# A softmax loop with VectorE's one-operand passes gathered in one block per step, GpSimd's two passes behind it, and stages one step later

## What is computed

```python
x_int = x / scale
x_int = x_int - x_int.max(axis=-1, keepdims=True)
x_int = jnp.maximum(x_int, n * x0_int)
q = jnp.floor(x_int / x0_int)
r = x_int - x0_int * q
z = r * (r + b_int) + c_int
exp_int = jnp.clip(jnp.floor(z * jnp.exp2(n - q)), 0.0, None)
exp_sum = exp_int.sum(axis=-1, keepdims=True)
sm = jnp.round(exp_sum / exp_int)
big = jnp.floor(jnp.log2(sm))
big = jnp.where(sm - jnp.exp2(big) >= jnp.exp2(big - 1.0), big + 1.0, big)
qlog = jnp.clip(big, 0.0, float(2 ** BITS_S - 1))
return jnp.where(big >= 16, 0.0, jnp.exp2(-qlog))
...
o = jnp.einsum('bhnm,bhmd->bhnd', attn, v)
```

## Time and profile before

| | |
|---|---|
| median of three runs | 1189.9 us |
| the profiled execution | 1189.11 us, its span 1187.3 us |
| busy: TensorE / VectorE / ScalarE / GpSimd | 803.7 / 883.3 / 499.1 / 515.9 us |
| softmax loop, roughly | 434 to 695 us of the span |
| granted TensorE clock, mean of the span | 0.718 |

### The profile page before, as it was taken

The page is one execution under the profiler, slowest core; times in us unless marked ns, Lnnn a source line. Parts: engine busy times, 40 slices in busy tenths (PEclk is TensorE's granted clock), DMA queues, the critical chain, the costliest instruction groups (busy, mean ns, idle before and its releaser), DMA issues.

```text
span 1187.3 us, 25829 instructions
## 1 busy us (share of the span) xinstructions
PE 803.7 (68%) x8714; PEld 613.7 (52%) x8714; DVE 883.3 (74%) x1781; ACT 499.1 (42%) x980; POOL 515.9 (43%) x413
## 2 busy tenths in 40 slices
PE   3898961576077625777778730600739999999998
PEld 2897961455044412444445430200627777777777
DVE  4324424899689969999999976699557777777776
ACT  2222201344454314666666632120415555555554
POOL 1120002587122006666666630633007666666665
PEclk9998995778555555555555555555559999999999
DMA  7544212000022111122112134000000000000000
GB/s 201 154 119 102 63 40 82 22 1 0 12 83 69 54 28 31 28 34 33 28 33 33 21 86 140 0 0 0 10 15 16 23 22 28 28 21 20 28 21 20
DMA packets 112975, 51.84 MB, mean 44 GB/s; under 512 B 75896, under 2 KB 107808, under 8 KB 112928
## 3 DMA queue, kind: packets, MB, share of 16 engines
q1 hardware_dynamic: 111600, 44.94, 15.6%
q0 software_dynamic: 1328, 6.30, 1.9%
HBM read 26.47 MB, written 6.68 MB: 28 GB/s over the span
## 4 chain that ended last, share of the span: by engine, by line
PE 50%; DVE 24%; issue 11%; SPq 5%; DMA 4%; ACT 3%; POOL 2%; DVEq 1%; POOLq 0%; ACTq 0%
PE ps L1267 46%; DVE R L1081 4%; DVE R L1088 2%; DMA R<-h_rows 2%; SPq L435 2%; DVE M L1002 2%; DVE M L1001 2%; DVE R L1094 1%; DVE R L1182 1%; PE ps L1338 1%; SPq L473 1%; ACT R L615 1%; DVE R L991 1%; DVE R L1191 1%; SPq L475 1%
## 5 line engine op out<-in xcount | busy, mean ns | idle before, releaser
L1267 PE MATMUL ps<-R 128*128 128x192 f16 (+9 forms) x3788 | 468.9, 276 | 78.7 <-DVE R L1094 61.3
L1267 PEld LDWEIGHTS ps<-R 128*128 128x128 f16 (+5 forms) x3788 | 356.2, 114 | 170.7 <-issue 77.0
L604 POOL TENSOR_TENSOR R<-R 128x256 f32<-128x256 f32 x238 | 195.5, 828 | 175.0 <-DVE R L1244 173.4
L615 ACT ACTIVATE R<-R,sc 128x884 int16<-128x884 f16 (+13 forms) x135 | 131.3, 1007 | 158.3 <-POOL R L547 41.6
L1267 PE MATMUL ps<-M 32*64 32x68 bf16 (+2 forms) x2048 | 127.0, 252 | 71.0 <-DMA M<-R 53.5
L1244 DVE TENSOR_TENSOR R<-R,ps 64x256 f32<-64x256 f32 (+1 forms) x272 | 113.9, 419 | 63.0 <-ACT R L789 43.7
L1267 PEld LDWEIGHTS ps<-M 32*64 32x64 bf16 (+2 forms) x2048 | 83.8, 136 | 128.8 <-issue 71.7
L789 ACT ACTIVATE R<-ps 128x256 f32<-128x256 f32 x238 | 91.3, 384 | 136.5 <-PE ps L1267 129.5
L612 ACT ACTIVATE R<-ps 68x896 bf16<-68x896 bf16 (+6 forms) x123 | 81.4, 665 | 141.9 <-PE ps L1338 53.2
L612 ACT ACTIVATE R<-R 128x256 f16<-128x256 f32 (+5 forms) x264 | 118.7, 451 | 32.4 <-POOL R L530 20.6
L1251 DVE TENSOR_TENSOR R<-R 128x256 f16<-128x256 f32 x238 | 112.8, 475 | 20.2 <-ACT R L612 18.1
(11 more groups left out here) (217 smaller groups left out, 1098.1 us busy)
## 6 DMA issues: line engine op xcount, KB each, us to landing
R<-in_x_dram SPq DMA_DIRECT2D x12, 576.0 KB, 10.7
M<-R SPq DMA_DIRECT2D x16, 260.0 KB, 2.4
M<-R SPq DMA_DIRECT2D x32, 130.0 KB, 2.1
R<-h_rows SPq DMA_DIRECT2D x4, 816.0 KB
R<-h_rows SPq DMA_DIRECT2D x1, 3264.0 KB, 13.1
R<-R SPq DMA_DIRECT2D x17, 192.0 KB, 2.5
out_dram<-R SPq DMA_DIRECT2D x17, 192.0 KB, 2.0
M<-R SPq DMA_DIRECT2D x128, 12.8 KB
```

The source lines that it names most:

```text
L604: pool.tensor_tensor(hs[0:rows, m % HB, :], hr[0:rows, m % HB, :], other, ALU.mult).then_inc(sem("squared"), 1)
L615: return act.activation(out_, in_, ACT.Identity, scale=scale, bias=bias)
L1267: return pe.matmul(o, a, b, start=start, stop=stop, skip_group_check=True)
```

## The change

Three lists of stages get another order and other lags. On VectorE the two small instructions of `totals` become a stage of their own, `shares`; it stands first, ahead of clamp, quotients and prob_bits. The large instruction of `totals`, `probabilities` and `weights` follow, then `weight_sums` and `distances`. `totals` moves from lag 2 to 3, `weights` from 1 to 2; `weight_sums` keeps lag 2 and now comes behind `weights`. On GpSimd `quotient_bits` moves from lag 2 to 3, so both passes of a group are in one step. On ScalarE `exponent` moves from lag 3 to the head of the list with lag 4. `PW` and `sq` get a second buffer, and `weights` also waits for `log2` of the group two before its own, since GpSimd reads that `wv` until then.

```diff
-        PW = r0(CW // 2, I16)
-        sq = r0(CW)
+        PW = [r0(CW // 2, I16) for _ in range(2)]
+        sq = [r0(CW) for _ in range(2)]
...
-            pipeline(pool, [(excess, 3), (quotient_bits, 2)], 32)
+            pipeline(pool, [(excess, 3), (quotient_bits, 3)], 32)
...
             def powers(g, par, half):
                 act.wait_ge(sem("quot"), g + 1)
-                wait(act, "w", g)
-
-                ident_(PW, Qq[par], scale=-128.0, bias=s1(A_PB)).then_inc(sem("power"), 1)
+                wait(act, "w", g - 1)
+
+                ident_(PW[par], Qq[par], scale=-128.0, bias=s1(A_PB)).then_inc(sem("power"), 1)
 
             def squares(g, par, half):
                 act.wait_ge(sem("rem"), g + 1)
-                wait(act, "w", g)
-                act.activation(sq, rem, ACT.Square, bias=s1(A_BH)).then_inc(sem("sq"), 1)
+                wait(act, "w", g - 1)
+                act.activation(sq[par], rem, ACT.Square, bias=s1(A_BH)).then_inc(sem("sq"), 1)
...
-            pipeline(act, [(evac_first, 5), (powers, 1), (squares, 1), (exponent, 3), (evac_o, 7), (evac_second, 5)], 32)
+            pipeline(act, [(exponent, 4), (evac_first, 5), (powers, 1), (squares, 1), (evac_o, 7), (evac_second, 5)], 32)
...
                 wait(dve, "excess", g - 1)
-
-                dve.scalar_tensor_tensor(flat(wv[par]), sq, s1(A_K0), PW.bitcast(BF16), ALU.add, ALU.mult).then_inc(sem("w"), 1)
+                wait(dve, "log2", g - 1)
+
+                dve.scalar_tensor_tensor(flat(wv[par]), sq[par], s1(A_K0), PW[par].bitcast(BF16), ALU.add, ALU.mult).then_inc(sem("w"), 1)
...
-            def totals(g, par, half):
+            def shares(g, par, half):
                 dve.wait_ge(sem("wsum"), g + 1)
                 ts(S[:, par, 1, :], S[:, par, 0, :], 1.0 / 3.0, None, ALU.mult).then_inc(sem("third"), 1)
                 ts(S[:, par, 2, :], S[:, par, 0, :], 2.0 / 3.0, None, ALU.mult).then_inc(sem("two_thirds"), 1)
+
+            def totals(g, par, half):
                 dve.wait_ge(sem("third"), g + 1)
                 wait(dve, "exponent", g - 1)
...
-            pipeline(dve, [(clamp, 1), (quotients, 1), (prob_bits, 4), (probabilities, 4), (weight_sums, 2), (totals, 2),
-                           (weights, 1), (distances, 0)], 32)
+            pipeline(dve, [(shares, 3), (clamp, 1), (quotients, 1), (prob_bits, 4), (totals, 3), (probabilities, 4),
+                           (weights, 2), (weight_sums, 2), (distances, 0)], 32)
```

## The result

The changed kernel takes 1252.9 us, the median of four runs (1252.12 to 1256.61), against 1191.84 for the kernel before beside it: ratio 1.051, 95% interval 1.0461 to 1.0559. It is slower. The forecast was 1266 us in a range of 1205 to 1280, of which 1252 to 1280 was called the forecast's own; the result lies at that inner range's lower end. The profiled execution took 1253.54 us, 64.4 more than the one of before (1189.11).

A forecast was written before the change was run, and what follows sets the result against it. VectorE's queue of passes was taken to bound the softmax loop. 1189.1 us plus 76.7 (full steps +70.6, last steps +7.6, first steps -1.5) gave 1265.8, rounded to 1266; range 1205 to 1280, forecast's own 1252 to 1280, chance 0.80.

The forecast's parts named there:

- the full step: Softmax loop, one VectorE step with all stages: 10.35 us against 7.83, 3.30 added and 0.78 taken away, +2.52.
- The block: VectorE's small passes, clamp, quotients and prob_bits together, no GpSimd pass beside them: gives back 0.36 + 0.42 = 0.78 us a step.
- The turns: Behind totals, GpSimd's two passes go ahead of queued probabilities and weights, which are held: 3.30 us a step added.
- Rivals 1, 2 and 3: 1: no or cheap holding, 1165, chance 0.07; 2: VectorE's queued pass wins, 1195, 0.06; 3: GpSimd's second pass late, 1207, 0.07.
- The Trainium skill's 2.6 cycles per element: GpSimd two-input passes, estimated 1.9 us for 884 elements; would add 0.4 us a step, some 11 us; not used.
- The mis-sized term: VectorE's weight_sums, distances, small passes, clamp, quotients and prob_bits behind the held passes: 4.00 us of the step.
- The sum: Steps 4 to 31: 28 x 2.52 = +70.6; last steps +7.6; first steps -1.5; total +76.7 us.
- The last steps: Loop end behind the last distances: 26.1 us against 18.5 in the old order, +7.6.
- the first steps: Loop start: distances' operands ready before GpSimd begins, thanks to later stages; -1.5 us, bounds 0 and -2.9.
- The stated cover of 3 us for the exponent: ScalarE's exponent waits for GpSimd, is done at 6.8, and prob_bits wants it at 9.9, so the added wait is free.

The follow-up runs named there:

- the last experiment: Changed kernel with GpSimd's loop passes cut to 2 columns, and prob_bits moved behind totals, directly in front of probabilities, which waits for it; measured once, 1156.9 us.

## Why the prediction was right

The mechanism was the forecast one, step for step; the size of the full step was 0.35 us too long. That is most of the 0.5 us that the forecast allowed itself, so the result stands close to where its own range ends: the profiled execution rose by 64.4 us, not by 76.7.

- **The block** gave back what was said: the small pass 0.53 to 0.17, clamp 0.87 to 0.44.
- **The turns.** GpSimd's first pass came 0.22 us behind the start of totals, not 0.13, and took 2.38, not 2.49; its end is the forecast one, since it follows the end of totals by 1.53 where the forecast's row has 1.51. Forecast were 2.57 us for probabilities and 2.94 for weights, measured 2.54 and 2.92. The runs without GpSimd's passes show that nothing else is in them, those with one pass that each has its own price, and the two with prob_bits moved that arrival alone decides. Rivals 1, 2 and 3 are refuted by the same rows: the passes are held, GpSimd's records are not longer than 2.88, and its second pass is queued before its turn. The Trainium skill (SBUF — State Buffer, Who interferes with whom) has the exclusion itself, that a VectorE instruction with two SBUF inputs contends with a GpSimd one that reads SBUF and the second blocks; the 2.54 us agree. Who of two that wait comes next, on which this kernel turned, is from the rows.
- **The Trainium skill's 2.6 cycles per element** (GPSIMD Engine Reference, Elementwise — side-by-side cycle accounting), an estimated 1.9 us, were rightly left for the row: L562 alone takes 1.67 us, L569 2.04, in the run with both passes behind weights (L565 and L572 there). Why the pass with the broadcast operand and 16-bit result is the shorter was not tried.
- **The mis-sized term** is the 4.00 us for the six stages behind weights, and the full step with it. By starts in the rows above, forecast against measured: weight_sums 1.10 and 0.99, distances 1.37 and 1.24, small passes 0.20 and 0.15, clamp 0.49 and 0.47, quotients 0.42 and 0.43, prob_bits 0.42 and 0.30: 4.00 and 3.58. Most of these terms are start-to-start times of the old order, and three of them (weight_sums, distances, prob_bits) hold a wait of the next pass on the one directly in front that the new order doesn't have: 0.11, 0.13 and 0.12 of the 0.42 us. For prob_bits the last experiment shows it, for the other two it is read from the same overlap of records. Against it weights is followed after 2.96, not 2.86, since weight_sums now waits for it. With 0.03 less for the first two the step is 10.00 instead of 10.35.
- **The sum.** The old step, over 28 of them, was (675.53 - 455.51) / 28 = 7.86 us by these rows of the kernel before, where the prediction took 7.83 from one step; the new one is (733.55 - 453.55) / 28 = 10.00 by the same line's rows.

```profile
455.51 1.32 DVE L1081 SCALAR_TENSOR_TENSOR R<-ps,sc,M 128x544 f16<-128x544 f32 x2
...
675.53 1.33 DVE L1081 SCALAR_TENSOR_TENSOR R<-ps,sc,M 128x544 f16<-128x544 f32 x2
```

So 28 x 2.14 = 60.0 where 70.6 was forecast. The last steps, from the start of distances to the end of probabilities, are 26.9 us against 19.9, +7.0 (forecast +7.6); the first steps gained 2.2 (forecast 1.5); what lies around the loop moved by -0.4. Together 64.4.

The stated cover of 3 us for the exponent held in the change: VectorE shows no idle time in its full steps. The run with both passes late used it up.

## What to carry to other kernels

If VectorE and GpSimd share a loop, list for each VectorE pass whether it can run beside a GpSimd pass. Here a reduction and a pass that reads PSUM could (2.24 us a step), one-operand passes and passes with two SBUF tensors could not, and GpSimd needed about 3.4. In each of the seven orders here that do all the work something was held, 0.8 us a step at the least. So put the free passes behind the one beside which GpSimd arrives, let no excluded pass be queued there, and check on which side of the next pass's start GpSimd arrives. Two excluded passes in a row did no harm in the kernel before (totals and weights), since GpSimd came during the last of them. A held pass is busy in the profile, so look for one line with two durations rather than for idle time.

## What was not expected of the hardware

- A pass that waits for the pass directly in front and reads its result starts 0.12 us later than one whose wait is long met: behind prob_bits 0.42 us after its start against 0.29 to 0.31, in all the kernels here. The Trainium skill (VectorE: DVE Perf Modes, The DRAIN you can't avoid) says that the next VectorE instruction doesn't start before the pipeline is empty, one that isn't held starting earlier, and that a semaphore after each costs nothing extra. Here the next record starts 0.08 us before the end of the one in front when it needn't wait, and 0.04 behind it when it must, so in this loop such a dependence is not free.
- A GpSimd pass on 2 columns takes 0.96 us in the record when it meets a two-operand VectorE pass, in the changed kernel without GpSimd's passes (the first row below). In the kernel before without them (the second) it takes 0.20 where no VectorE pass is under way. So some three quarters of the 0.96 are waiting, and it ends at 601.89, 0.05 behind the end of probabilities (600.77 + 1.07).

```profile
600.93 0.96 POOL L569 TENSOR_TENSOR R<-R 128x2 int32<-128x2 int32 x1
```
```profile
446.54 0.20 POOL L569 TENSOR_TENSOR R<-R 128x2 int32<-128x2 int32 x1 [16.43 <-DVE R L1117]
```

So a GpSimd record's length says little of its work in such a place.
